# A graph attention layer and an eight-expert layer on one core: drain order, first block load and padding moved

## What is computed

```python
def gnn(h, adj, W, a):
    Wh = jnp.matmul(h, W)
    e = Wh @ a[:D] + jnp.swapaxes(Wh @ a[D:], 1, 2)
    e = jnp.where(e > 0, e, 0.2 * e)
    e = jnp.where(adj > 0, e, -jnp.inf)
    return jax.nn.elu(jnp.matmul(softmax(e), Wh))

def ffn(x, Wg, bg, W1, b1, W2, b2):
    topk_scores, topk_idx = jax.lax.top_k(einsum('bsd,ed->bse', x, Wg) + bg, 2)
    combine = sum(softmax(topk_scores)[..., None] * one_hot(topk_idx, 8))
    for e in range(8):
        h = relu(x @ W1[e].T + b1[e])          # 128 -> 512
        out += combine[..., e:e+1] * (h @ W2[e].T + b2[e])
    return out

x = x + gnn(layernorm(x), adj, W, a)
x = x + ffn(layernorm(x), Wg, bg, W1, b1, W2, b2)
```

## Time and profile before

| | us |
|---|---|
| median of 3 runs | 476.25 (475.17 to 477.98) |
| the profiled execution | 476.44 |
| its span, first to last instruction | 474.6 |
| PE busy / DVE / ACT / POOL, of the span | 405.9 / 368.5 / 320.4 / 288.7 |
| token stage, to the first transposes of an expert block | 204.1 |

### The profile page before, as it was taken

One profiled execution on the slowest core, in us unless ns is written; L12 is line 12 of the kernel. 1 busy time (PEld: TensorE's weight loads), 2 busy tenths in 40 slices (PEclk: granted clock), 3 DMA queues, 4 the chain that ended last, 5 costly groups with the idle time before them and its releaser, 6 DMA issues.

```text
span 474.6 us, 9446 instructions
## 1 busy us (share of the span) xinstructions
PE 405.9 (86%) x2256; PEld 309.4 (65%) x2256; DVE 368.5 (78%) x1415; ACT 320.4 (68%) x760; POOL 288.7 (61%) x283
## 2 busy tenths in 40 slices
PE   2988898988888988679999999999999999999500
PEld 1656666666566664358878788787887878888300
DVE  6489999999999998546768677686776867777982
ACT  2578788888878985047767777677776777777300
POOL 0001777777767777674656766576565675566763
PEclk9999999999989998979999999999999999999855
DMA  5586343333323333342433322323223332277699
GB/s 141 161 307 211 91 118 102 96 97 97 106 79 107 104 115 95 113 121 70 129 107 90 102 64 86 106 84 108 65 84 106 90 104 64 84 261 241 221 304 298
DMA packets 55647, 60.85 MB, mean 128 GB/s; under 512 B 7616, under 2 KB 40768, under 8 KB 55360
## 3 DMA queue, kind: packets, MB, share of 16 engines
q1 hardware_dynamic: 36736, 35.15, 24.9%
q0 software_dynamic: 8704, 17.97, 11.4%
q10 hardware_dynamic: 10176, 7.39, 5.0%
HBM read 27.28 MB, written 24.81 MB: 110 GB/s over the span
## 4 chain that ended last, share of the span: by engine, by line
PE 56%; DVE 18%; issue 8%; POOL 8%; DMA 5%; ACT 3%; DVEq 1%; SPq 1%; POOLq 0%; ACTq 0%
PE bank L1218 8%; PE bank L1201 8%; PE bank L1215 7%; PE bank L1202 7%; PE bank L1205 7%; PE bank L1216 7%; POOL expert_slots L489 7%; PE bank L1181 4%; PE bank L1189 3%; DVE xn L832 2%; PE bank L1142 2%; PE bank L1140 2%; DVE score L795 2%; DVE bn L815 2%; DVE x_all L804 2%
## 5 line engine op out<-in xcount | busy, mean ns | idle before, releaser
L489 POOL DMA_INDIRECT expert_slots<-rows,slot_i x128 | 128.3, 1003 | 84.0 <-DMA rows<-xn 40.7
L1014 DVE CAST hh<-z 128x512 fp32r<-128x512 f32 x36 | 18.0, 499 | 57.5 <-ACT z L664 57.5
L679 ACT ACTIVATE yb<-bank,b_sb 128x512 f32<-128x512 f32 x36 | 24.8, 689 | 53.2 <-PE bank L1218 53.2
L1215 PE MATMUL bank<-hh,w_hi 128*128 128x512 f32 x144 | 60.4, 420 | 0.0
L506 POOL DMA_INDIRECT moe_rows<-hrelu,ysi x40 | 42.1, 1053 | 29.8 <-DVE ysi L1004 18.9
L1201 PE MATMUL bank<-xh,w_hi 128*128 128x512 f32 x144 | 58.7, 408 | 0.7 <-ACT xh L643 0.7
L1218 PE MATMUL bank<-hl,w_hi 128*128 128x512 f32 x144 | 58.3, 405 | 0.0
L1202 PE MATMUL bank<-xh,w_lo 128*128 128x512 f32 x144 | 57.3, 398 | 0.0
L1205 PE MATMUL bank<-xl,w_hi 128*128 128x512 f32 x144 | 57.1, 397 | 0.0
L1216 PE MATMUL bank<-hh,w_lo 128*128 128x512 f32 x144 | 56.7, 394 | 0.0
L506 POOL DMA_INDIRECT moe_rows<-hexp,ysi x40 | 41.3, 1031 | 22.8 <-DVE ysi L1004 13.4
(11 more groups left out here) (154 smaller groups left out, 1041.4 us busy)
## 6 DMA issues: line engine op xcount, KB each, us to landing
xs<-expert_slots SPq DMA_DIRECT2D x34, 260.0 KB
rows<-xn SPq DMA_DIRECT2D x32, 256.0 KB
x_all<-x SPq DMA_DIRECT2D x16, 256.0 KB, 3.0
w_raw<-w_t SPq DMA_DIRECT2D x2, 2048.0 KB, 11.5
w_raw<-moe_rows SPq DMA_DIRECT2D x16, 256.0 KB, 3.9
out<-x_all ACTq DMA_DIRECT2D x16, 256.0 KB, 4.8
w_hi<-moe_rows SPq DMA_DIRECT2D x9, 256.0 KB, 3.5
expert_slots<-pad_rows ACTq DMA_DIRECT2D x8, 260.0 KB, 2.7
```

Source lines behind the costliest of these rows:

```text
L489: nc.gpsimd.indirect_dma_start(out=slots, out_offset=bass.IndirectOffsetOnAxis(ap=slot_i[q][:, k * SUB + j:k * SUB + j + 1], axis=0), in_= ...
L679: nc.scalar.activation(yb[:, :], ps_y[:, :], ACT.Identity, bias=b2_sb[:, e:e + 1]).then_inc(yb_ok, 1)
L1215: nc.tensor.matmul(ps_y[:, :], w2_hi[:, e, c, :], hh[:, c, :], start=c == 0, stop=False)
```

## The change

In the drain, VectorE no longer runs `step` but two functions written out by hand, `drain` and `drain_rows`. The operations themselves were put into small functions (`add_counts`, `add_bases`, `write_slots`, `elu_sum`, `residual`, `second_stats`, `next_tokens`, `second_var`, `choose`, `choose_both`, `newton_1` to `newton_3`, `second_shift`, `gap_sum`, `first_weight`, `second_weight`, `row_ids`), with the same bodies and waits as before; `step` calls them in its old order in all earlier steps. On TensorE the rank became `rank`, in step 17 behind the `xn2` transposes, and its fills now also stand in step 16. On ScalarE the exponential of step 17 moves behind `xn2`. `due_groups` does without the last column, which `due_last` adds. ScalarE loads block 0; SyncE starts at block 1; expert 0 has two blocks at least (`least`). GpSimd writes two pads for expert 0, counted on `rows_out[0]`. The computation of `pairs_ok` and `late_i` on VectorE moves behind the first four turns of the expert stage.

```diff
-CAP = TOKENS + GROUP
+CAP = TOKENS + 2 * GROUP
...
-FILL_STEP, FILL_NORM, FILL_DRAIN, FILL_TABLE = 3, 8, 7, 22
+FILL_STEP, FILL_NORM, FILL_DRAIN, FILL_TABLE = 3, 8, 5, 14
...
+        def draining(t):
+
+            return isinstance(t, int) and t == GROUPS + 1
+
+        def by_steps(eng, step, end=GROUPS + STAGES - 1):
...
+        def rows_due(eng, cell):
+
+            due = eng.value_load(cell, min_val=2, max_val=GROUPS)
+            eng.wait_ge(rows_out[0], ((due + 1) >> 1) * (16 * 2 * SUB) + (due >> 4) * 32)
+            eng.sem_inc(due_met, 1)
+            eng.wait_ge(rows_out[1], (due >> 1) * (16 * 2 * SUB))
+            eng.sem_inc(due_met, 1)
...
-            sp.wait_ge(due_ok, 3)
+            sp.wait_ge(due_ok, 4)
             sp.wait_ge(table_ok, 1)
 
             bounds = [0, block_bound(sp, 0)]
-            with sp.Fori(0, bounds[1]) as i:
+            with sp.Fori(1, bounds[1]) as i:
                 own = nc.s_assert_within(i, 0, FULL - 1, skip_runtime_bounds_check_because="an expert has at most TOKENS tokens")
-                due = sp.value_load(due_i[0:1, bass.ds(own, 1)], min_val=2, max_val=GROUPS)
-                for q in range(2):
-                    sp.wait_ge(rows_out[q], ((due + (1 - q)) >> 1) * (16 * 2 * SUB))
-                    sp.sem_inc(due_met, 1)
-                sp.wait_ge(pad0_out, (due >> 4) * 16 + 1)
-                sp.sem_inc(due_met, 1)
+                rows_due(sp, due_i[0:1, bass.ds(own, 1)])
                 load_block(sp, own * GROUP, i)
             for q in range(2):
                 sp.wait_ge(rows_out[q], 16 * 2 * SUB * (GROUPS // 2))
@@ -492,6 +498,13 @@
                                 in_=rows[q][:, k, j, :], in_offset=None).then_inc(rows_out[q], 16)
 
             by_steps(pool, step)
+            pool.wait_ge(table_ok, 1)
+            pool.wait_ge(pads_ok, 1)
+            pool.wait_ge(rows_out[0], 16 * 2 * SUB * (GROUPS // 2))
+            n = pool.value_load(count_i[0:1, 0:1], min_val=0, max_val=TOKENS)
+            for k in range(2):
+                nc.gpsimd.dma_start(slots[bass.ds(n + k * GROUP, GROUP), :].rearrange("(p s) r -> p s r", s=SUB),
+                                    pad_rows[:, :, :]).then_inc(rows_out[0], 16)
             pairs, rest = pairs_and_rest(pool)
...
+                if gl is not None and draining(t):
+                    gap_exp(gl)
...
             by_steps(act, step)
-            act.wait_ge(table_ok, 1)
+            act.wait_ge(due_ok, 4)
+            rows_due(act, due_i[0:1, 0:1])
+            load_block(act, 0, 0)
             act.wait_ge(pads_ok, 1)
             act.wait_ge(c_b1, 16)
             act.wait_ge(c_b2, 16)
@@ -648,9 +668,9 @@
                 act.dma_start(slots[bass.ds(n + e * CAP, GROUP), :].rearrange("(p s) r -> p s r", s=SUB),
                               pad_rows[:, :, :]).then_inc(out_ok, 16)
 
-            pad(0, pad0_out)
+            act.wait_ge(table_ok, 1)
+            pad(1, pads_out)
             bounds = [0, block_bound(act, 0)]
-            pad(1, pads_out)
             round_x(0)
...
+            nc.vector.memset(least[:, 1:E], 1.0)
+            nc.vector.memset(least[:, 0:1], 2.0)
...
+                dve.wait_ge(count_ok, GROUPS - 2)
+                nc.vector.tensor_tensor(short[:, :, :], cst[:, C_FULL:C_END][:, :, None].to_broadcast([P, FULL, GROUPS - 1]),
+                                        count_f[:, None, 0:GROUPS - 1, 0].to_broadcast([P, FULL, GROUPS - 1]), ALU.is_gt
+                                        ).then_inc(due_ok, 1)
                 dve.wait_ge(due_ok, 1)
                 nc.vector.tensor_reduce(due_f[:, :], short[:, :, :], AX, ALU.add).then_inc(due_ok, 1)
                 dve.wait_ge(due_ok, 2)
-                nc.vector.tensor_scalar(due_i[:, :], due_f[:, :], 2.0, None, ALU.max).then_inc(due_ok, 1)
+                nc.vector.tensor_scalar(due_f[:, :], due_f[:, :], 2.0, None, ALU.max).then_inc(due_ok, 1)
+
+            def due_last():
+
+                dve.wait_ge(due_ok, 3)
+                dve.wait_ge(count_ok, GROUPS - 1)
+                nc.vector.scalar_tensor_tensor(due_i[:, :], cst[:, C_FULL:C_END], count_f[:, GROUPS - 1, 0:1], due_f[:, :],
...
+            def drain():
+
+                t = GROUPS + 1
+                q, m = t % 2, t // 2
+                gx, gl, gr = GROUPS - 1, GROUPS - 2, GROUPS - 3
+                add_counts(gr)
+                add_bases(gr)
+                write_slots(gr, q, m)
+                due_groups()
+                elu_sum(gx)
+                residual(gx)
+                second_stats(gx)
+                next_tokens(gl)
+                second_var(gx)
+                newton_1(gx)
+                newton_2(gx)
+                newton_3(gx)
+                second_shift(gx)
+                choose(gl)
+                choose_both(gl)
+                gap_sum(gl)
+                first_weight(gl, q, m)
+                second_weight(gl, q)
+                row_ids(gl, q)
+                low_halves(t - LOW)
+                gl, gr = gl + 1, gr + 1
+                add_counts(gr)
+                due_last()
+                add_bases(gr)
+                next_tokens(gl)
+                choose(gl)
+                choose_both(gl)
+                write_slots(gr, 1 - q, (t + 1) // 2)
+                gap_sum(gl)
+                add_counts(gr + 1)
+
+            def drain_rows():
+
+                t = GROUPS + 2
+                q, m = t % 2, t // 2
+                gl = GROUPS - 1
+                add_bases(gl)
+                first_weight(gl, q, m)
+                second_weight(gl, q)
+                row_ids(gl, q)
+                write_slots(gl, 1 - q, m)
+
+            by_steps(dve, step, GROUPS + 1)
+            drain()
 
...
+            nc.vector.tensor_tensor(blocks_m[:, :], blocks_r[:, :], least[:, :], ALU.max).then_inc(blocks_ok, 1)
...
-                                    ).then_inc(blocks_ok, 1)
...
 
+            keep_meta(0)
+            low_x(0)
+            halve_hidden(0)
+            for b in range(BUFS):
+                turn(b, b, 0)
+            nc.vector.tensor_scalar(until_i[:, E:E + 1], until_f[:, E - 1:E], 0.5, 0.75 - FULL, ALU.mult, ALU.add
+                                    ).then_inc(blocks_ok, 1)
+            dve.wait_ge(blocks_ok, 5)
+            nc.vector.tensor_copy(pairs_f[:, :], until_i[:, E:E + 1]).then_inc(blocks_ok, 1)
+            dve.wait_ge(blocks_ok, 6)
+            nc.vector.scalar_tensor_tensor(blocks_f[:, 0:1], pairs_f[:, :], -2.0, until_f[:, E - 1:E], ALU.mult, ALU.add
+                                           ).then_inc(blocks_ok, 1)
+            dve.wait_ge(blocks_ok, 7)
+            nc.vector.tensor_scalar(until_i[:, E + 1:E + 2], blocks_f[:, 0:1], float(BUFS * QUADS + 1), None, ALU.subtract
+                                    ).then_inc(pairs_ok, 1)
             nc.vector.tensor_scalar(late_f[:, :, :], count_f[:, 2:GROUPS:2, E - 2:E], float(GROUP - 1), 1.0 / GROUP, ALU.add, ALU.mult
                                     ).then_inc(late_ok, 1)
             dve.wait_ge(late_ok, 1)
...
 
+            def rank(t, gl):
+
+                if isinstance(t, int) and t >= GROUPS:
+                    pe.wait_ge(z_ok, GROUPS)
+                    fill(ps_z, FILL_DRAIN)
+                pe.wait_ge(chosenb_ok, gl + 1)
+                if later(gl):
...
@@ -1159,6 +1295,8 @@
                         pe.wait_ge(xn2_ok, SUB * gx + (j + 1))
                         last = nc.tensor.transpose(tiles(ps_t3)[:, j, :], xn2[q][:, j, :], ident)
                     last.then_inc(xn2_ps, 1)
+                if gl is not None and draining(t):
+                    rank(t, gl)
                 if gx is not None:
                     pe.wait_ge(xn2_t_ok, gx + 1)
                     if later(gx):

```

More of the change, by code:

```diff
@@ L172, in gnn_moe_kernel @@
         blocks_m = sb("blocks_m", [P, E])
+        least = sb("least", [P, E])
         ones8 = sb("ones8", [P, E])
@@ L351, in by_steps @@
                     step(2 * m + q, [2 * m + (q - n) for n in range(STAGES)], q, m)
-            for t in range(GROUPS - 2, GROUPS + STAGES - 1):
+            for t in range(GROUPS - 2, end):
                 at(t)
@@ L594, in step @@
                     nc.scalar.copy(xn1_t[:, :], ps_t1[:, :]).then_inc(xn1_t_ok, 1)
-                if gl is not None:
-                    act.wait_ge(gap_ok, gl + 1)
-                    nc.scalar.activation(gap_e[:, :], gap[:, :], ACT.Exp).then_inc(gape_ok, 1)
+                if gl is not None and not draining(t):
+                    gap_exp(gl)
                 if g1 is not None:
@@ new lines, in write_slots @@
+            def write_slots(gr, q, m):
+                dve.wait_ge(slotp_ok, gr + 1)
+                if later(m - 2):
+                    dve.wait_ge(rows_out[q], 16 * 2 * SUB * (m - 2))
+                with nc.allow_low_precision(reason="one term of a sum is a slot's number, the others are zero"):
```

(2 more changed lines are left out.)

323 lines of the change are left out of this document (163 added, 160 removed).

## The result

The changed kernel takes 474.35 us (median; 472.36 to 477.6) where the kernel before takes 476.29 (475.17 to 478.27), 20 runs each. The ratio is 0.9949, with a 95% interval of 0.9936 to 0.9963: 1.9 to 2.4 us faster, by about 0.5%. The profiled execution took 475.31, of which 473.6 is the span; before it was 476.44 and 474.6. So the two traces are only 1.0 apart: the changed one is from an execution 0.96 above its own median. The kernel before took 563 to 570 us there, so only ratios and places in the trace are read from them.

The account below looks back on a forecast made before the run. TensorE alone was taken to bound the expert stage, with time to be had at the handover's standstill and low clock. From 476.44, less 4.4 at T4, plus 1.7 for the clock: 473.7 profiled, 473.5 median; range 468.5 to 477.2.

Parts of the forecast that it names:

- The fills in step 16: TensorE's five extra fills ahead of the rank: 2.2 us on the path at half clock, 1.1 at full clock.
- The drain: VectorE's new order: `u` at 183.9 (182.8 at the low end), last choice at 193.7, last rank at 195.9.
- T0: TensorE's transposes of expert 0's first block: at 199.9 after ScalarE's load, 4.2 us earlier.
- T4: TensorE's transposes of expert 0's last block: at 226.0, between 224.9 and 227.2, a gain of 4.4 us.
- T1: TensorE's transposes of expert 0's second block, loaded by SyncE: at 204.0, 7.1 us earlier.
- Block 4: Expert 0's last block waits for all scatters and two GpSimd pads; half of the 2.3 us slot delay was counted.
- The rival in which a pad costs four scatters: Each GpSimd pad takes 4.2 us, T4 comes at 230.7, time 479.7, slower; chance 0.12.
- the one in which nothing holds block 4: GpSimd does not hold expert 0's last block: the gain is 7.1 us, time 469.2; chance 0.17.
- The clock behind the hold: TensorE's 2.65 us standstill ahead of T4 brings one low-clock stretch of 3.4 us, costing 1.7.
- GpSimd's late start: GpSimd's first sends near 240.0, so `weigh(4)` waits 1.8 us; taken as covered by VectorE's idle time, cost 0.
- late sends not covered: Rival in the expert stage: GpSimd's late sends cost their full 1.8 us, time 475.3; chance 0.10.
- it doesn't do what it says: Rival: ScalarE's load comes no earlier than SyncE's did, T0 stays, time 476.3; chance 0.08.

Follow-up runs that it names:

- the run with all three: Changed kernel with GpSimd's count read behind its loop, group 14's slots written ahead of the last choice, expert 0's pads from ScalarE: 471.4 us, ratio 0.9896.
- the late read: Changed kernel with GpSimd's read of the two counts moved from ahead of its first send to behind its loop: 473.8 us, ratio 0.9932.
- the run with SyncE's load: Changed kernel with block 0 loaded by SyncE in its loop again and nothing loaded by ScalarE: 476.56 us, ratio 1.000.
- the run with two loads: The run with all three, but ScalarE also loads block 1 and SyncE writes expert 0's two pads: 471.41 us, ratio 0.9879.
- all eight on disturbed chips: Eight runs of the changed kernel with one or two edits, on chips whose engines stood still for nothing the trace shows: ratios 0.9931 to 1.0407 where given.
- the early read: GpSimd reads the counts ahead of its first send, as in the changed kernel; six such runs on disturbed chips were 2.2 to 4.1% slower than the kernel before.

## Why the prediction was right

The forecast was 473.5 and the median is 474.35, inside the range, and faster by 0.5%. The mechanism was the one forecast: early first load, block 4 held by the pads behind the last scatter, a low clock behind the hold. By its steps:

- **The fills in step 16** were put at 2.2 on the path. They took 1.90 at low clock and moved VectorE's step by 1.1 (179.70 in the kernel before, 180.80 here), since in the kernel before VectorE had been busy until then itself. In two other traces of these versions they ran at full clock, 1.24, in two they took 1.91 and 1.96. With the due table `u` came at 182.56, not 183.9, just below the low end.
- **The drain** behind that was right in its differences: `xn2` to the last choice 5.05 (5.3 forecast), choice to last rank 2.21 (2.2), rank to table 1.85 (1.65). All of it lay 1.4 to 1.6 earlier than forecast, with the table at 196.12 in place of 197.55. The load was at 194.40 in place of 196.35, since ScalarE took 1.19 and not 1.5 from its last exponential to it.
- **T0** was forecast at 199.9 by the load. It came at 198.78, and by the fills: I had kept the clock at 1.00 there. At full clock, 3.18 for the fills as in the run with all three, it would have been 197.5. This cost nothing at T4.
- **T1**: 203.22 against 204.0. It was not SyncE's chain that set it but T0 and TensorE's own work behind it, 4.44 (4.43 with the late read, where the load had landed 0.45 ahead of T1); the forecast had 3.92 for that (6.98 less 3.06).
- **Block 4.** T4 = 226.45 against 226.0, by errors that cancel: the mechanism was right, and that the number is so near is luck. The second scatter of group 14 came at 198.39, where the forecast puts it at 198.5: the group's first was 1.1 earlier than forecast (195.18, not 196.3), but the gap did not swallow half of the late slots; it came in full, 2.24 of 2.46. From there to the last scatter it was 19.71 (198.39 to 218.10), where it had been 18.14: three of them took 1.48 or 1.49 and not 0.97. That is 1.6 too late. Behind the last scatter's start the path to T4 was 8.35 and not 9.4: the pads took 0.6 each, with no pause between them, where 1.27 was taken, and the load 2.58, not 3.40; against that, the last scatter took 1.42, and the second pad landed 3.2 behind its issue (2.7 taken). The rival in which a pad costs four scatters is dead: one costs less than one scatter. So is the one in which nothing holds block 4. The Trainium skill's slower first byte for GpSimd's transfers (DMA: Bandwidth & Descriptors, Specifications) speaks the same way as the 3.17 here against a median of 2.4 for ScalarE's pads in the same trace; the estimate worked out from it was 0.4 later, and the pad landed 0.5 later than I had taken. With other traffic beside each, one such transfer does not settle it.
- **The clock behind the hold**: 1.7 forecast, 1.62 measured. That the stretch would be as long as the one at 177.1 was a guess from that one row.
- **GpSimd's late start** is the term that was mis-sized: 0 forecast, 0.95 measured between T7 and T8. The first send came at 241.07, not 240.0, so `weigh(4)` waited 2.38, not 1.8. From the first send to the landing of block 0 the forecast had 6.7, of which the four sends make 5.7; the other 1.0 has no row behind it, and 6.84 was measured. The cover was 1.5, not 1.6 or more: of 2.38, 0.9 came through; of 2.80 in the run with SyncE's load 1.6 did, a cover of 1.2. I had set a mean idle time per block against a wait just above it and called that covered. Of the later blocks' waits (0.31, 0.88) nothing is seen. The rival *late sends not covered* gave 475.3; the truth, 474.35, is midway.
- **That it doesn't do what it says** is out: undone, the early load costs 2.2 us.

The sum by measured terms of the profiled executions: 3.80 at T4, less 1.67 up to T5, 0.06 up to T7, 0.95 up to T8 and 0.12 up to the end, is the 1.0 of the spans. The forecast for that execution was 473.7, and it took 475.31; the medians differ by 1.94. The executions spread over 5 us, so how near the median came to 473.5 says little about the terms. One place where executions differ is the drain: the clock was low there in some traces (the changed kernel's at 193.5, the run with two loads at 194 to 200) and not in others.

## What to carry to other kernels

When a transfer is made early, follow what the same edit makes late: here 7.7 us won at the second block shrank to 1 in the trace through delays on GpSimd, which has 8% of the chain of waits in the kernel before. One of them, the late sends, went when one line was moved. The other two, slots and pads, went together. A register read belongs where its value is first used: GpSimd read two counts at 239, some 160 us ahead of where the version with the late read does (399), and everything queued behind that read began 20 us late. Cover is to be set against the wait at its own block, with its remainder counted, not a mean against a sum. And an engine may be held by something other than the number it is said to need: SyncE's load gained little from an earlier table, as its copies of the last group ended no sooner.

## What the runs showed that was not expected

- The gap of 2.2 us behind the first scatter of group 14 stands at one place in GpSimd's code: 2.46 before, 2.24, 2.24, 2.21, 2.24 in four changed versions, 2.24 in all eight on disturbed chips, 1.84 in the version with two loads, wherever the scatter itself lay. The Trainium skill (Runtime: NRT & Kernel Launch, Instruction fetch mechanics) has instructions come in blocks and the crossing "mostly hidden"; whether this gap is such a crossing no run here shows, and if it is, it was not hidden.
- A low clock in the drain does not follow from TensorE's wait for the last choice alone. A wait of 1.88 (late read), 1.98 (changed kernel) and 2.03 (two loads) stood ahead of 14 fills that took 4.51, 4.43 and 6.09; one of 1.78 (all three) and one of 2.03 (SyncE's load) stood ahead of fills at full clock, 3.18, the latter here:

```profile
193.99 0.19 PE L1228 MATMUL bank<-chosen_b,before_b 128*128 128x32 bf16 x1 [2.03 <-DVE chosen_b L872]
...
194.20 3.18 PE L1218 MATMUL bank<-mask_b,ident_b 128*128 128x512 bf16 x14
```

What else decides is open. It moved T0 by 1.3 in the changed kernel and by 1.4 with two loads, more than the late sends cost.
- Scatters of 128 rows took 0.97 in most cases, and 1.42 to 1.49 four times between 205 and 219 us in the changed kernel; in the run with the late read none did there, and one did in each of the other three on undisturbed chips. These moved the end of the scatters by up to 1.9 us. The cause is open.
- On the disturbed chips the loops of the routing stage stood for 4 to 6 us a step, and the kernels with the early read, which costs 0.9 us elsewhere, were 12 to 23 us slower than the kernel before. The two versions with the late read lost nothing against the kernel before.
